# Parts of q and k copied from SBUF to SBUF once a turn instead of through DRAM, with indirect stores, gathers and the ternary layer at other places, in a two-layer transformer kernel

## The chip, the cores and the metric

The kernel runs on one core of a Trainium2 chip. The metric is the device time of one launch in microseconds (us), the median of several runs. The code names the engines so: PE (TensorE, matmuls), DVE (VectorE), ACT (ScalarE), POOL (GpSimd), SP (SyncE, which only issues DMAs here).

## What is computed

Input x is 16 sequences of 512 tokens of 256 numbers. Four residual layers follow each other:

```
x = x + attention0(layernorm(x))   # 16 heads of 16, rotary q and k, window of 128 keys, softmax, output weights
x = x + experts(layernorm(x))      # 8 experts, each token goes to 2 of them: silu(a) * b, gates from a softmax
x = x + attention1(layernorm(x))   # 16 heads of 16, xpos rotary, causal over all 512, biases
x = x + ternary(layernorm(x))      # x @ w.T with w quantised to -1, 0, 1 times a scale
```

The attention scores need nearly float32 accuracy, while the score matmuls take bf16 operands. So q and k are each split into three bf16 parts that add up to the float32 value, and six products of parts are summed by one matmul with a contraction of 6 x 16 = 96 rows.

## The kernel before

The program has three stages. `pipeline` (lines 106 to 1034) runs twice, in the first launch stage as attention0 with the routing of the experts (`routed`, its tiles are a_..., about 0 to 1060 us), and last as attention1 with the sum of the experts' outputs in front and the ternary layer behind (`mixed`, about 2000 to 3335 us). Between them stands `experts`, which the change doesn't touch.

`pipeline` works on one sequence a turn, and several sequences are in the pipeline at once. In turn i the softmax part runs for sequence i (steps "T": the transposed scores k times q plus mask on PE, exp on ACT; steps "PV": probabilities times v on PE), the maxima of the rows for sequence s = i+1 (steps "S": q times k on PE, then the row minimum of the negated scores on DVE, line 839), layer norm, transposition and the projections to q and k for sequence m = i+2, and the output side (o = i-1). The function `turn(i)` (lines 148 to 200) gives each step a position between 0 and 1 in its turn; `merged` sorts them, and every engine runs its own steps in that one order. So a step that waits on an engine holds up all steps behind it there. PE runs the T, PV and S steps, the product to v (`v`), two transpositions of the output (`flip`, line 1017, and `back`, line 1023), the output product (`out`, line 1032), the transposition of the next input (`turn`, line 898), the projections (`project`, line 885) and the transposition of the row maxima (`minus`, line 977).

The parts of q and k of sequence m (a = 0 is q, a = 1 is k) come into the tile `parts` [128, 2, 3, 2, 512] in bf16: 128 partitions are 8 dimensions times 16 heads, 3 parts, 2 halves of the head. The first two parts are casts on ACT (lines 611 and 614), with subtractions on POOL (lines 548 and 552). The S and T matmuls want the 96 rows (which part, which half, which of 8 dimensions) on partitions and the heads along the free axis, in `qst` and `kst` [98, 16, 512], two buffers of each. This change of layout goes through DRAM: the step `store` (lines 461 to 468) writes the parts to `parts_d` in 3 DMAs for q and 6 for k (the order of the parts differs, `STORED`), and the step `stack` (lines 469 to 478) reads them back as 96 partitions, for a group of 4 heads at a time: 8 DMAs of 384 KB a sequence, each of 96 rows of 4 KB. The stacks of groups 0 to 2 stand at 0.70, 0.74 and 0.78 of the turn and that of group 3 at its end; each waits until the T steps of that group of sequence m-2 have left the buffer. The S step of each group waits for its own semaphore `stack_loaded`. The row maxima go into rows 96 and 97 of `qst` the same way, in two DMAs through `nmax_d` (lines 479 to 486).

The S steps of a turn stand evenly between 0.03 and 0.97 (28 of them in attention0, 44 in attention1).

POOL issues the indirect DMAs. In attention0 the 8 `scatter` DMAs of a sequence (line 525) write the normed tokens to the experts' input; they stand at 0.97 of the turn after the sequence's T steps and wait for the row numbers that DVE works out (line 810, position 0.9475). In attention1 the 8 `gather` DMAs (line 532) fetch the experts' outputs in two lots of 4, at 0.35 and 0.81 of a turn, into one tile `yg`; the DVE steps `mix` (line 690) add them to x, lot by lot, and wait for a whole lot of 4 (semaphore `gathered`). The second lot's `mix` stands at 0.94 to 0.985, the statistics of that sequence (line 674) at the start of the next turn.

Of the kernel before, what the change touches and what calls it, by code (L numbers as in the profile page):

```python
# [105 lines left out]
def pipeline(nc, name, x_in, x_out, w_all, w_out, tables, biases, window, scale, consts, routed, mixed, ternary_w):  # L106
# [18 lines left out]
    parts_d = nc.dram_tensor(f"{name}_parts_dram", [2, 2, NR, 2, P, T], BF16, kind="Internal").ap()  # L125
    nmax_d = nc.dram_tensor(f"{name}_nmax_dram", [2, 2, H, T], BF16, kind="Internal").ap()
# [21 lines left out]
    def turn(i):  # L148
# [11 lines left out]
        if 0 <= o < B:  # L160
# [3 lines left out]
            out += [(0.16 + 0.02 * t, ("stats2", o, t)) for t in range(NT)] + [(0.235, ("aggr2", o))]  # L164
            if routed:
                out += [(0.28 + 0.02 * t, ("norm2", o, t)) for t in range(NT)]
                out += [(0.15, ("y", o)), (0.50, ("turn2", o, 0)), (0.52, ("turn2", o, 1)), (0.58, ("score", o)),
                        (0.66, ("exp2", o)), (0.79, ("place", o)), (0.97, ("scatter", o))]
                out += [(0.615 + 0.0175 * k, ("gates", o, k)) for k in range(20)]
            else:  # L170
                out += [(0.27 + 0.015 * t, ("norm2", o, t)) for t in range(NT)]
                out += [(0.345, ("turn2", o, 0)), (0.36, ("turn2", o, 1)), (0.49, ("last", o, 0)), (0.51, ("last", o, 1)),
                        (0.515, ("final", o, 0)), (0.535, ("final", o, 1)), (0.54, ("y", o))]
        if 0 <= s < B:
            lo, hi = 0.03, 0.97
            out += [(lo + (hi - lo) * (k + 0.5) / NS, ("S", s, k // NSG, k % NSG)) for k in range(NS)]
            out += [(0.01, ("v", s)), (0.035, ("vcopy", s, 0)), (0.055, ("vcopy", s, 1)), (0.54, ("minus", s, 0, 0)), (0.68, ("minus", s, 0, 1))]
        for n, at in ((m, -0.5),) * (m == 0) + ((m + 1, 0.55),) * (0 <= m + 1 < B):
            out.append((at, ("load", n)))
            if mixed:  # L180
                out += [(at - 0.2, ("gather", n, 0)), (at + 0.26, ("gather", n, 1))]
                out += [(at + 0.19 + 0.02 * t, ("mix", n, 0, t)) for t in range(NT)]
                out += [(at + 0.39 + 0.015 * t, ("mix", n, 1, t)) for t in range(NT)]
            else:
                out += [(at + 0.25 + 0.02 * t, ("stats", n, t)) for t in range(NT)] + [(at + 0.33, ("aggr", n))]
        if biases and 0 <= m < B:
            out.append((0.50, ("shift", m)))
        if 0 <= m < B:
            if mixed:
                out += [(0.005 + 0.02 * t, ("stats", m, t)) for t in range(NT)] + [(0.075, ("aggr", m))]  # L190
                out += [(0.125 + 0.015 * t, ("norm", m, t)) for t in range(NT)]
            else:
                out += [(0.03 + 0.02 * t, ("norm", m, t)) for t in range(NT)]
            out += [(0.20, ("turn", m, 0)), (0.215, ("turn", m, 1))]
# [8 lines left out]
    for i in range(-2, B + 1):  # L203
# [6 lines left out]
    with ctx:  # L210
# [197 lines left out]
        parts_stored = [sem(f"parts_stored{i}") for i in range(2)]  # L408
        stack_loaded = [[sem(f"stack_loaded{i}{g}") for g in range(NG)] for i in range(2)]
        nmax_stored = sem("nmax_stored")  # L410
# [14 lines left out]
        gathered = sem("gathered")  # L425
# [26 lines left out]
        def _(sp):  # L452
            for st in order:
# [7 lines left out]
                elif st[0] == "store":  # L461
                    m, a = st[1:]
                    sp.wait_ge(part2_done, 2 * m + a + 1)
                    for r, (p0, np_) in enumerate(STORED[a]):
                        src = parts[:, a, p0:p0 + np_]
                        dst = parts_d[m % 2, a, STORED_AT[a][r]:STORED_AT[a][r] + np_]
                        sp.dma_start(dst.rearrange("r b p n -> p (r b) n"), src.rearrange("p r b n -> p (r b) n"))\
# [1033 lines left out]
```

## Time and profile before

| what | us |
|---|---|
| median of 3 runs | 3323.2 |
| lowest and highest run | 3319.46, 3323.53 |
| the profiled execution's own time | 3336.26 |
| span of its trace | 3334.6 |

The profiled execution is 13.1 us longer than the median of the runs, and 1.7 us of its time lie outside the span. In the rows, a timeline row has the start and duration in us, the engine, the line, the operation with its tiles (out<-in) and the number merged into the row; square brackets give the idle time of the engine before it and what ended it. "SPq" is the queue in which SP issues. "PEclk" is the granted clock of PE as a share of 2.4 GHz, and the DMA share is the mean busy share of 16 DMA engines.

### The profile page before, as it was taken

The page shows a single profiled execution, that of the slowest core. Times are in us where ns is not written, and L with a number is a line of the kernel's source. Part 1 is how long each engine was busy: PE and PEld are TensorE (multiplying, and loading weights), DVE is VectorE, ACT ScalarE, POOL GpSimd, SP SyncE. Part 2 cuts the span into 40 slices and gives each one's busy share as a digit, 9 for nine tenths or more (in the row PEclk, how much of TensorE's full clock was granted, in tenths as well). Part 3 has the DMA queues.
Part 4 walks back from the last instruction along what each step waited for, and adds up shares of the span by engine and source line. Part 5 has one row for each costly group of instructions (what it writes and reads, how often), then busy time and mean ns, then how long its engine had stood idle before and what let it go on. Part 6 is the DMA issues. An engine that isn't in the chain of part 4 may idle for free. (4 is left out here: it accounts for less than half of the span.)

```text
span 3334.6 us, 52247 instructions
## 1 busy us (share of the span) xinstructions
PE 2627.1 (79%) x17657; PEld 1777.4 (53%) x17830; DVE 1940.5 (58%) x6550; ACT 1463.5 (44%) x2485; POOL 1140.8 (34%) x919
## 2 busy tenths in 40 slices
PE   2788788888886488888888882588888888887887
PEld 2455555555553377777777771244444444444444
DVE  4667677577673344555554443566666656666661
ACT  1445455454453244344443431145555554455554
POOL 2334434444322233333333323333443333333310
PEclk8899999999997698999999995589998998899998
DMA  4544534435431333333333323533334443333330
GB/s 113 152 123 147 153 110 149 151 110 167 139 97 47 137 133 132 132 123 125 120 130 131 132 82 98 165 96 103 107 108 137 126 126 112 103 103 102 103 90 14
DMA packets 240529, 394.13 MB, mean 118 GB/s; under 512 B 26432, under 2 KB 190272, under 8 KB 235072
## 3 DMA queue, kind: packets, MB, share of 16 engines
q1 hardware_dynamic: 222272, 336.94, 33.3%
q0 software_dynamic: 18048, 54.54, 4.9%
q8 instruction: 115, 1.88, 0.2%
q14 instruction: 94, 0.77, 0.1%
HBM read 230.84 MB, written 160.56 MB: 117 GB/s over the span
## 5 line engine op out<-in xcount | busy, mean ns | idle before, releaser
L839 DVE CUSTOM_DVE_ANT_0 a_junk<-a_bank,a_smask 128x256 bf16<-128x256 f32 (+3 forms) x2048 | 812.6, 435 | 523.9 <-PE a_bank L969 514.6
L636 ACT ACTIVATE a_pr<-a_bank 128x512 f32<-128x512 f32 (+1 forms) x1152 | 635.6, 574 | 690.8 <-PE a_bank L890 507.8
L969 PE MATMUL a_bank<-a_kst,a_qst 96*128 96x256 bf16 (+3 forms) x2048 | 459.5, 299 | 203.8 <-DVE a_nmax L839 147.3
L1255 POOL TENSOR_TENSOR e_wl<-e_w_raw,e_wh 128x2048 fp32r<-128x2048 f32 x80 | 279.0, 3488 | 578.6 <-ACT e_wh L1292 578.6
L991 PE MATMUL a_bank<-a_qst,a_kst 98*128 98x256 bf16 (+3 forms) x2048 | 434.8, 289 | 26.5 <-ACT a_pr L636 23.7
L969 PEld LDWEIGHTS a_bank<-a_kst,a_qst 96*128 96x128 bf16 x2048 | 169.7, 102 | 451.2 <-DVE a_nmax L839 268.1
L1009 PE MATMUL a_bank<-a_pr,a_va 128*32 128x256 f32 (+3 forms) x4096 | 360.1, 429 | 47.3 <-ACT a_pr L636 43.2
L1340 PE MATMUL e_bank<-e_xh,e_wh 128*128 128x512 f32 x640 | 277.9, 434 | 111.5 <-DVE e_gf L1313 103.2
L1313 DVE SCALAR_TENSOR_TENSOR e_gf<-e_bank,e_b,e_sa 128x512 f32<-128x512 f32 x160 | 119.8, 749 | 325.7 <-ACT e_sa L1276 325.1
L890 PE MATMUL a_bank<-a_mask,a_identb 128*128 128x128 bf16 (+2 forms) x979 | 284.8, 291 | 0.0
L1317 DVE TENSOR_TENSOR e_gl<-e_gf,e_gh 128x512 fp32r<-128x512 f32 x160 | 211.0, 1319 | 112.7 <-ACT e_gh L1281 112.7
L1340 PE MATMUL e_bank<-e_xl,e_wh 128*128 128x512 f32 x640 | 271.6, 424 | 0.0
L1340 PE MATMUL e_bank<-e_xh,e_wl 128*128 128x512 f32 x640 | 270.0, 422 | 0.0
L991 PEld LDWEIGHTS a_bank<-a_qst,a_kst 98*128 98x128 bf16 x2048 | 180.6, 100 | 149.2 <-ACT a_pr L636 74.5
L1276 ACT ACTIVATE e_sa<-e_bank,e_b 128x512 f32<-128x512 f32 x160 | 109.6, 685 | 283.4 <-PE e_bank L1340 283.4
L1340 PEld LDWEIGHTS e_bank<-e_xh,e_wh 128*128 128x128 f32 x640 | 131.9, 206 | 154.2 <-DVE e_gf L1313 108.9
L532 POOL DMA_INDIRECT a_yg<-ys,a_yrow x128 | 123.9, 968 | 195.8 <-DVE a_xt L690 136.6
L514 POOL TENSOR_SCALAR a_lean<-a_mv 128x4 f32<-128x4 f32 x32 | 7.7, 240 | 529.2 <-DVE a_mv L702 529.2
L1009 PEld LDWEIGHTS a_bank<-a_pr,a_va 128*32 128x32 f32 x4096 | 84.7, 110 | 181.7 <-issue 89.4
L1354 PE MATMUL e_bank<-e_wh,e_gh 128*128 128x256 f32 x640 | 178.1, 278 | 2.9 <-DVE e_gl L1317 2.9
L1354 PE MATMUL e_bank<-e_wh,e_gl 128*128 128x256 f32 x640 | 177.9, 278 | 0.0
L1354 PE MATMUL e_bank<-e_wl,e_gh 128*128 128x256 f32 x640 | 177.8, 278 | 0.0
(172 smaller groups left out, 5255.0 us busy)
## 6 DMA issues: line engine op xcount, KB each, us to landing
a_parts_dram<-a_parts SPq DMA_DIRECT2D x224, 256.0 KB, 3.9
a_qst<-a_parts_dram SPq DMA_DIRECT2D x128, 384.0 KB, 9.8
a_kst<-a_parts_dram SPq DMA_DIRECT2D x128, 384.0 KB, 10.7
e_w_raw<-in_we SPq DMA_DIRECT2D x40, 1024.0 KB, 6.3
a_parts_dram<-a_parts SPq DMA_DIRECT2D x32, 768.0 KB, 3.8
e_xg<-xs SPq DMA_DIRECT2D x40, 512.0 KB, 3.8
e_w_raw<-in_we SPq DMA_DIRECT2D x40, 512.0 KB, 8.2
ys<-e_yt POOLq DMA_DIRECT2D x40, 512.0 KB, 7.8
```

The costliest lines, as they stand in the source:

```text
L532: pool.indirect_dma_start(yg[:, t, :], None, ys, bass.IndirectOffsetOnAxis(ap=yrow[:, k, m * NT + t:m * NT + t + 1], axis=0))\
L636: nc.scalar.activation(pr[b][:, h:h + per, :], TB_[at % 2][:, 0:per * w].rearrange("p (h w) -> p h w", h=per), ACT.Exp, scale=scale).then_ ...
L839: last = nc.vector.tensor_tensor_reduce(junk[:, at % 2, j * w:(j + 1) * w], SB_[at % 2][:, j * w:(j + 1) * w], smask[:, T - w:T], scale=-1 ...
L890: return nc.tensor.matmul(out, identb[:, :], rhs, start=False, stop=True, skip_group_check=True)
L969: last = nc.tensor.matmul(out[:, j * w:(j + 1) * w], q[0:ROWS, hh, qb * P:(qb + 1) * P], k[0:ROWS, hh, k0:k0 + w], start=True, stop=True)
L991: nc.tensor.matmul(out[:, j * w:(j + 1) * w], k[0:AUG, hh, b * P:(b + 1) * P], q[0:AUG, hh, q0:q0 + w], start=(j == 0), stop=False, skip_g ...
L1009: last = nc.tensor.matmul(PVB[32 * j:32 * (j + 1), q0:q0 + w], va[i % 2][:, b, (g * HG + j) * VW:(g * HG + j) * VW + 32], pr[b][:, j, :], ...
L1255: nc.gpsimd.tensor_tensor(part(wl[m.slot]), part(w_raw[m.slot]), part(wh[m.slot]).bitcast(F32), ALU.subtract).then_inc(wl_done, 1)
L1313: nc.vector.scalar_tensor_tensor(gf[f % 2][:, :], BB[f % 2][:, :], b1[s.slot][:, FC + f:FC + f + 1], sa[f % 2][:, :], ALU.add, ALU.mult).t ...
L1317: nc.vector.tensor_tensor(gl[s.slot][:, f, :], gf[f % 2][:, :], gh[s.slot][:, f, :].bitcast(F32), ALU.subtract).then_inc(gl_done, 1)
L1340: last = nc.tensor.matmul(out[:, :], first(w[s.slot])[:, kc, col:col + P], x[s.slot][:, kc, :], start=(p == 0), stop=(p == 3 * KC - 1))
L1354: last = nc.tensor.matmul(YB[n][:, (t % 2) * D:(t % 2 + 1) * D], x[s.slot][:, f, t * P:(t + 1) * P], second(w[s.slot])[:, f, :], start=(p ...
```

## The change

The parts go from `parts` straight to `qst` and `kst`. One DMA copies one part and half, 128 partitions of 1 KB, to 8 partitions with 16 heads of 1 KB each: 12 DMAs for q and 12 for k a sequence, 24 of 128 KB. They all stand at the end of the turn, wait until all T steps of sequence m-2 are done, and raise one semaphore; the first S step of the sequence waits for all 24. The S steps stand between 0.20 and 0.98. The row maxima take one DMA instead of two. `parts_d` and `nmax_d` go. The scatters, which stood at 0.97 of a turn, stand one by one at 0.115 to 0.213 of the next. In attention1 the load of x moves from 0.55 to 0.435, the gathers stand one by one at 0.27 to 0.345 and 0.57 to 0.645, each of the 4 rows of `yg` with a semaphore of its own, the second lot of `mix` at 0.72 to 0.78, the statistics at 0.80 to 0.86 of the same turn, and the ternary layer goes forward (`last` from 0.49 to 0.37, `y` from 0.54 to 0.42).

```diff
             if routed:
                 out += [(0.28 + 0.02 * t, ("norm2", o, t)) for t in range(NT)]
-                        (0.66, ("exp2", o)), (0.79, ("place", o)), (0.97, ("scatter", o))]
+                        (0.66, ("exp2", o)), (0.79, ("place", o))]
...
-                out += [(0.27 + 0.015 * t, ("norm2", o, t)) for t in range(NT)]
-                out += [(0.345, ("turn2", o, 0)), (0.36, ("turn2", o, 1)), (0.49, ("last", o, 0)), (0.51, ("last", o, 1)),
-                        (0.515, ("final", o, 0)), (0.535, ("final", o, 1)), (0.54, ("y", o))]
+                out += [(0.235 + 0.015 * t, ("norm2", o, t)) for t in range(NT)]
+                out += [(0.31, ("turn2", o, 0)), (0.325, ("turn2", o, 1)), (0.37, ("last", o, 0)), (0.385, ("last", o, 1)),
+                        (0.40, ("final", o, 0)), (0.415, ("final", o, 1)), (0.42, ("y", o))]
+        if routed and 0 <= i - 2 < B:
+            out += [(0.115 + 0.014 * k, ("scatter", i - 2, k)) for k in range(2 * NT)]
         if 0 <= s < B:
-            lo, hi = 0.03, 0.97
+            lo, hi = 0.20, 0.98
...
-            out += [(0.01, ("v", s)), (0.035, ("vcopy", s, 0)), (0.055, ("vcopy", s, 1)), (0.54, ("minus", s, 0, 0)), (0.68, ("minus", s, 0, 1))]
+            out += [(0.01, ("v", s)), (0.035, ("vcopy", s, 0)), (0.055, ("vcopy", s, 1)), (0.63, ("minus", s, 0, 0)), (0.75, ("minus", s, 0, 1))]
-        for n, at in ((m, -0.5),) * (m == 0) + ((m + 1, 0.55),) * (0 <= m + 1 < B):
+        for n, at in ((m, -0.5),) * (m == 0) + ((m + 1, 0.55 if routed else 0.435),) * (0 <= m + 1 < B):
             out.append((at, ("load", n)))
             if mixed:
-                out += [(at - 0.2, ("gather", n, 0)), (at + 0.26, ("gather", n, 1))]
-                out += [(at + 0.19 + 0.02 * t, ("mix", n, 0, t)) for t in range(NT)]
-                out += [(at + 0.39 + 0.015 * t, ("mix", n, 1, t)) for t in range(NT)]
+                for t in range(NT):
+                    out += [(at - 0.165 + 0.025 * t, ("gather", n, 0, t)), (at + 0.125 + 0.02 * t, ("mix", n, 0, t)),
+                            (at + 0.135 + 0.025 * t, ("gather", n, 1, t)), (at + 0.285 + 0.02 * t, ("mix", n, 1, t)),
+                            (at + 0.365 + 0.02 * t, ("stats", n, t))]
+                out.append((at + 0.465, ("aggr", n)))
...
             for a in range(2):
-                p = 0.27 + 0.13 * a
+                p = 0.24 + 0.19 * a if mixed else 0.27 + 0.13 * a
-                        (p + 0.15, ("part", m, a, 0)), (p + 0.21, ("part", m, a, 1)), (p + 0.27, ("store", m, a))]
-            out += [(0.70 + 0.04 * g, ("stack", m, g)) for g in range(NG - 1)] + [(1.0, ("stack", m, NG - 1))]
+                        (p + 0.15, ("part", m, a, 0)), (p + 0.21, ("part", m, a, 1)), (0.995 + 0.001 * a, ("stack", m, a))]
...
                 elif st[0] == "stack":
                     m, a = st[1:]
                     sp.wait_ge(part2_done, 2 * m + a + 1)
+                    sp.wait_ge(t_done, max(0, (m - 1) * NS))
+                    dst = (qst, kst)[a][m % 2]
                     for r, (p0, np_) in enumerate(STORED[a]):
+                        for p in range(np_):
+                            for b in range(2):
+                                at = ((STORED_AT[a][r] + p) * 2 + b) * (DH // 2)
+                                sp.dma_start(dst[at:at + DH // 2, :, :], parts[:, a, p0 + p, b, :])\
+                                    .then_inc(stack_loaded[m % 2], 16)
                 elif st[0] == "minus" and st[3] == 1:
...
+                    sp.dma_start(qst[s % 2][ROWS:AUG, half * H // 2:(half + 1) * H // 2, :], nmt[half][:, :])\
                         .then_inc(nmax_loaded[s % 2][half], 16)
...
                 elif st[0] == "scatter":
-                    r = st[1]
+                    r, k, t = st[1], st[2] // NT, st[2] % NT
                     pool.wait_ge(rows_done, r + 1)
...
-                    pool.wait_ge(mixed_in, NT * (2 * m + k))
+                    pool.wait_ge(mixed_in, max(0, NT * (2 * m + k - 1) + t + 1))
...
-                        act.wait_ge(parts_stored[a], 16 * len(STORED[a]) * m)
+                        if m:
+                            act.wait_ge(stack_loaded[(m - 1) % 2], 16 * 4 * NR * ((m - 1) // 2 + 1))
                         nc.scalar.copy(parts[:, a, 0], qk[:, a]).then_inc(part0_done, 1)
...
-                        dve.wait_ge(gathered, 16 * NT * (2 * m + k + 1))
+                    dve.wait_ge(gathered[t], 16 * (2 * m + k + 1))
...
-                    if n == 0:
-                        pe.wait_ge(stack_loaded[s % 2][g], 32 * (s // 2 + 1))
+                    if (g, n) == (0, 0):
+                        pe.wait_ge(stack_loaded[s % 2], 16 * 4 * NR * (s // 2 + 1))
```

## Rows read from the trace of the kernel before

**Rows 1.** The page: busy time of each engine, share of the span, instructions.

```profile
PE 2627.1 (79%) x17657; PEld 1777.4 (53%) x17830; DVE 1940.5 (58%) x6550; ACT 1463.5 (44%) x2485; POOL 1140.8 (34%) x919
```

**Rows 2.** Windows: one turn of attention0 in two stretches, one of attention1.

```profile
core 0: us, PE busy (x) PEld busy (x) DVE busy (x) ACT busy (x) POOL busy (x), PEclk, DMA share, GB/s
582.90:606.90 24.00, 17.89 (x128) 13.18 (x131) 9.54 (x50) 9.50 (x19) 9.12 (x11) 0.86 0.62 194
606.90:644.30 37.40, 33.66 (x293) 20.58 (x297) 33.22 (x150) 21.22 (x38) 15.73 (x14) 1.00 0.33 104
...
2520.40:2544.50 24.10, 18.48 (x123) 11.50 (x123) 12.05 (x49) 10.63 (x21) 1.71 (x4) 0.86 0.37 91
2544.50:2594.80 50.30, 43.44 (x303) 23.73 (x305) 36.76 (x130) 27.44 (x50) 25.20 (x21) 0.93 0.39 119
```

**Rows 3.** Timeline of PE, attention0: the drain of one turn.

```profile
568.11 0.38 PE L969 MATMUL a_bank<-a_kst,a_qst 96*128 96x256 bf16 x2
568.32 0.38 PE L991 MATMUL a_bank<-a_qst,a_kst 98*128 98x256 bf16 x2
...
582.49 0.38 PE L890 MATMUL a_bank<-a_mask,a_identb 128*128 128x512 bf16 x1
...
595.77 1.12 PE L1023 MATMUL a_bank<-a_ident,a_on 128*128 128x128 f32 x4 [5.47 <-issue]
...
597.65 3.71 PE L1032 MATMUL a_bank<-a_wo,a_ot 128*128 128x256 f32 x8 [0.34 <-ACT a_ot L652]
...
601.86 1.89 PE L1032 MATMUL a_bank<-a_wo,a_ot 128*128 128x256 f32 x8
...
606.55 0.39 PE L977 MATMUL a_bank<-a_identb,a_nparts 128*16 128x128 bf16 x4
```

**Rows 4.** Timeline of POOL, attention0: the first and the last of 8 scatters.

```profile
585.05 1.09 POOL L525 DMA_INDIRECT xs<-a_rn,a_row  x1 [0.67 <-DVE a_row L810]
...
594.03 0.96 POOL L525 DMA_INDIRECT xs<-a_rn,a_row  x1 [0.30 <-issue]
```

**Rows 5.** Timeline of DVE, attention1: the wait for the second lot of gathers.

```profile
2527.75 0.88 DVE L690 SCALAR_TENSOR_TENSOR a_xt<-a_yg,a_gate,a_xt 128x256 f32<-128x256 f32 x2 [6.64 <-issue]
```

**Rows 6.** Groups of DVE, attention1, ten turns (2312.6 to 3060.1 us).

```profile
L690 DVE SCALAR_TENSOR_TENSOR a_xt<-a_yg,a_gate,a_xt 128x256 f32<-128x256 f32 x80 | 36.8, 481 | 62.8 <-issue 62.8
...
L674 DVE BATCH_NORM_STATS2 a_stats<-a_xt 128x6 f32<-128x256 f32 x40 | 15.9, 418 | 0.0
```

**Rows 7.** Windows of rows 2, line 839 alone: DVE busy, PEclk, DMA.

```profile
582.90:606.90 24.00, 5.68 (x34) 0.86 0.62 194
...
2520.40:2544.50 24.10, 6.43 (x29) 0.86 0.37 91
```

**Rows 8.** Windows (columns of rows 2): DMA at the parts' store, then the maxima's load and store.

```profile
574.00:578.00 4.00, 3.67 (x47) 2.06 (x48) 3.90 (x26) 1.76 (x4) 0.00 (x0) 1.00 1.08 381
...
548.70:549.05 0.35, 0.35 (x4) 0.26 (x3) 0.35 (x3) 0.00 (x0) 0.26 (x2) 1.00 0.11 47
547.15:547.40 0.25, 0.25 (x4) 0.10 (x1) 0.25 (x3) 0.00 (x0) 0.00 (x0) 1.00 0.27 66
```

**Rows 9.** Timeline of SP's queue: 16 loads of 16 KB in a row.

```profile
3.91 7.38 SPq L333 DMA_DIRECT2D a_wo<-in_wo  x16
```

**Rows 10.** Line 482, the store of the row maxima, 16 KB.

```profile
DMA to landing us min/median/max: 1.4/2.0/4.4
```

**Rows 11.** Timeline: the last part and the first S, attention0, then attention1.

```profile
53.94 2.12 POOL L552 TENSOR_TENSOR a_parts<-a_qk,a_parts 128x1024 bf16<-128x1024 f32 x1 [1.16 <-ACT a_parts L614]
69.78 1.04 PE L969 MATMUL a_bank<-a_kst,a_qst 96*128 96x128 bf16 x6 [20.85 <-DMA a_kst<-a_parts_dram]
...
2083.63 2.12 POOL L552 TENSOR_TENSOR a_parts<-a_qk,a_parts 128x1024 bf16<-128x1024 f32 x1 [1.16 <-ACT a_parts L614]
2099.49 1.03 PE L969 MATMUL a_bank<-a_kst,a_qst 96*128 96x128 bf16 x6 [26.90 <-DMA a_kst<-a_parts_dram]
```

More of the change, by code:

```diff
@@ L163, in turn @@
                     (0.145, ("add", o, 1))]
-            out += [(0.16 + 0.02 * t, ("stats2", o, t)) for t in range(NT)] + [(0.235, ("aggr2", o))]
+            if routed:
+                out += [(0.16 + 0.02 * t, ("stats2", o, t)) for t in range(NT)] + [(0.235, ("aggr2", o))]
+            else:
+                out += [(0.155 + 0.015 * t, ("stats2", o, t)) for t in range(NT)] + [(0.21, ("aggr2", o))]
             if routed:
@@ L188, in turn @@
         if 0 <= m < B:
[L189 to L194, printed above, removed]
+            out += [(0.03 + 0.02 * t, ("norm", m, t)) for t in range(NT)]
+            out += [(0.18 if mixed else 0.20, ("turn", m, 0)), (0.195 if mixed else 0.215, ("turn", m, 1))]
             for a in range(2):
-                p = 0.27 + 0.13 * a
+                p = 0.24 + 0.19 * a if mixed else 0.27 + 0.13 * a
                 out += [(p, ("project", m, a)), (p + 0.04, ("rope", m, a, 0)), (p + 0.065, ("rope", m, a, 1)),
-                        (p + 0.15, ("part", m, a, 0)), (p + 0.21, ("part", m, a, 1)), (p + 0.27, ("store", m, a))]
-            out += [(0.70 + 0.04 * g, ("stack", m, g)) for g in range(NG - 1)] + [(1.0, ("stack", m, NG - 1))]
+                        (p + 0.15, ("part", m, a, 0)), (p + 0.21, ("part", m, a, 1)), (0.995 + 0.001 * a, ("stack", m, a))]
         return out
     order = []
-    for i in range(-2, B + 1):
+    for i in range(-2, B + 2):
         order += merged([turn(i)])
@@ L407, in pipeline @@
         x_loaded = [sem(f"x_loaded{i}") for i in range(RING)]
-        parts_stored = [sem(f"parts_stored{i}") for i in range(2)]
-        stack_loaded = [[sem(f"stack_loaded{i}{g}") for g in range(NG)] for i in range(2)]
-        nmax_stored = sem("nmax_stored")
+        stack_loaded = [sem(f"stack_loaded{i}") for i in range(2)]
         nmax_loaded = [[sem(f"nmax_loaded{i}{half}") for half in range(2)] for i in range(2)]
@@ L424, in pipeline @@
         scattered = [sem(f"scattered{i}") for i in range(2)]
-        gathered = sem("gathered")
+        gathered = [sem(f"gathered{t}") for t in range(NT)]
         mixed_in = sem("mixed_in")
@@ L460, in _ @@
                         .then_inc(x_loaded[m % RING], 16)
[L461 removed]
+                elif st[0] == "stack":
                     m, a = st[1:]
                     sp.wait_ge(part2_done, 2 * m + a + 1)
+                    sp.wait_ge(t_done, max(0, (m - 1) * NS))
+                    dst = (qst, kst)[a][m % 2]
                     for r, (p0, np_) in enumerate(STORED[a]):
[L465 to L478 removed]
+                        for p in range(np_):
[3 more added lines that the diff above has]
+                                    .then_inc(stack_loaded[m % 2], 16)
                 elif st[0] == "minus" and st[3] == 1:
```

39 lines of the change are left out of this document (10 added, 29 removed).

## The prediction

> **What bounds the kernel now.** The page first: PE is busy for 79% of the span, DVE for 58%, and no engine is full [rows 1]. So a share is no answer, and I cut a turn at the point the change touches: the end of the last T step of a sequence, since from there the copies may start. The first stretch runs from there to the transposition of the maxima at position 0.205; I call it the drain, and it is where the change takes the S steps out. The rest of the turn is the main stretch. In attention0 they take 24.0 and 37.4 us (61.4 a turn), in attention1 24.1 and 50.3 (74.4) [rows 2]. In the main stretch of attention0 DVE is busy 33.2 of 37.4 us and PE 33.7: both are nearly full, and the stretch can't shrink much. In the drain PE is busy 17.9 of 24.0 us at a mean granted clock of 0.86, in attention1 18.5 of 24.1 at 0.86, and DVE about half or less. Here the time lies open.
>
> Why: in attention0 PE stands idle for 5.47 us before line 1023, put down to nothing in the trace, and afterwards works at 1.2 GHz: the same eight records of line 1032 take 3.71 us and, a little later, 1.89 [rows 3]. The gap lies inside the 8 scatters on POOL, from 585.05 to 595.0 us [rows 4], which meet the last stack loads. In attention1 DVE waits 6.64 us for the second lot of gathers [rows 5], 62.8 us in ten turns [rows 6], with S steps queued behind, and PE runs dry. The loads themselves end no wait but the first one of each layer [rows 11].
>
> **What the change removes.** Six S steps leave the drain of attention0 and nine that of attention1. On PE one takes 0.21 us (568.11 to 568.32 [rows 3]), so 1.3 and 1.9 us. On DVE line 839 takes 5.68 and 6.43 us there [rows 7]. PE's necessary drain is its busy time, less what the low clock cost (0.14 of 24 us: 3.4), less these: 17.9 - 3.4 - 1.3 = 13.2 and 18.5 - 3.4 - 1.9 = 13.2 us. With about 1 us of short waits between ACT and PE I take 14 for both. That needs the two waits above gone. The gathers of attention1 leave the turn's end (to 0.65 at the latest, their `mix` 0.075 of a turn, 5 us, later), so the 6.64 us go. In attention0 the scatters don't in fact move: POOL has nothing between its last norm step at 0.88 and them, and their only wait, for the row numbers, ends at 0.95 in either kernel. What changes is what they meet: copies that stay inside SBUF instead of loads. I take the idle time as gone, and keep the other case as a rival.
>
> **What it adds: the copies.** The first S waits for all 24, PE is in order, and so T and PV steps queue behind it. Three prices, after the last T:
> - Issue. 16 small loads in a row took 7.38 us of SP, 0.46 each [rows 9]; 24 take 11.1 us. Nothing that is due is behind them on SP: the maxima's second half is issued at 0.205 and needed at 0.5.
> - Data. A busy DMA engine moved 381 / (16 x 1.08) = 22.0 GB/s in pieces of 1 KB [rows 8]. How many engines share a copy into 8 partitions no row shows, but the load into 2 partitions kept 0.11 x 16 = 1.8 engines busy [rows 8], so I take one for each partition: 8 engines. 3.146 MB / (8 x 22.0) = 17.9 us. With 16 engines it is 8.9, less than the issue.
> - Fixed. The shortest store of 16 KB took 1.4 us to land [rows 10].
>
> So the copies take 17.9 + 1.4 = 19.3 us; below, 11.1 + 1.4 = 12.5 (16 engines), above, see the third rival. I take 19.3, since the row with 2 partitions is nearest. It is more than PE's 14: the drain becomes 19.3 us, set by the copies.
>
> **The main stretch.** It gets the S steps and, in attention1, four `mix` at 0.481 and four statistics at 0.418 us [rows 6]. DVE there: 33.2 + 5.0 = 38.2 us, and 36.8 + 5.7 + 3.6 = 46.1 (one S of about 0.7 us stays in the drain). At the fullness of attention0's stretch, 33.2 / 37.4 = 0.89, that is 43 and 52; full, 38.2 and 46.1. I take 41 and 50: near the upper ends, the second helped by the 3.5 us that the clock of 0.93 cost it [rows 2].
>
> **The small edits at nothing.** The maxima lose a store and a wait, hidden by half a turn of T steps. The parts' store to DRAM goes; POOL and ACT wait for the copies of the turn before, over by 0.39. The ternary steps and `y` come earlier; what waits for `y` is only the load, needed a quarter of a turn on. If those covers went, PE would see some 2 us of landing.
>
> **The start of each layer.** From the last part to the first S now 69.78 - 56.06 = 13.7 us, and 99.49 - 85.75 = 13.7 [rows 11]; the part ends 2.12 after its start. With the copies 19.3: +5.6 twice.
>
> **Sum.** Attention0: 19.3 + 41 = 60.3 against 61.4, -1.1. Attention1: 69.3 against 74.4, -5.1. Fifteen full turns of each have copies, S and T: 15 x -6.2 = -93, plus 11 is -82 us. On the profiled execution's 3336.3 that gives 3254, and as the median of the runs is 13.1 lower, 3241.
>
> **Rivals.** Each by the same sum.
> - *All 16 engines share a copy.* Then it takes 12.5 us and PE's 14 set the drain: 55 and 64, -16.8 a pair, -252 and 2 less at the starts: 3069. For: with issue spread over 11 us the placing of S at 0.20 would just fit. Against: the two-partition row. Chance 0.17.
> - *The scatter gap stays.* Drain of attention0 24.0 - 1.3 = 22.7, a turn 63.7 (+2.3); attention1 as before: -42 + 11 = -31: 3292. Chance 0.10.
> - *Neighbouring partitions get in each other's way (slower).* All 8 target partitions of a copy are neighbours. The maxima's store reads 16 neighbouring partitions, and there an engine moved 66 / (16 x 0.27) = 15.3 GB/s instead of 22.0 [rows 8]. At that pace: 3.146 MB / (8 x 15.3) = 25.7, plus 1.4 is 27.1. Turns 68.1 and 77.1: +6.7 + 2.7, x 15 = 141, and 27 at the starts: 3491. The sign turns where the copies take 21.9 us. Against: the pair of engines that wrote to 2 neighbours moved 47 / 1.76 = 26.7 GB/s each. Chance 0.22.
> - *They block each other wholly.* If four neighbours share the pace of one engine at its best, a copy runs at 2 x 26.7 GB/s: 58.9 + 1.4 = 60.3 us, turns 101 and 110, +1137 and 93: 4553. For it speaks only the 16-partition row, and weakly; engines that fall out of step would reach other partitions. Chance 0.08. The Trainium skill states this as a rule (SBUF — State Buffer, "Door 1: The DMA port swizzle"): four neighbouring partitions hang on one port of 27.2 GB/s, so 8 give 54 GB/s. By it the copies take 58 + 1.4 us and this case is the forecast. The trace's pair of writers went past it over 16 KB, which is too short to settle a stream.
> - *DVE bounds the main stretch.* S squeezed into 0.78 of the turn makes it 45.1 and 55: +3.0 and -0.1: +43 + 11: 3377. Chance 0.08.
> - That the change does nothing measurable, cases in between: 0.05.
>
> **How the numbers follow.** The forecast has 0.30, with a range of its own of 3190 to 3290. Faster (beyond 0.2%, 7 us, about what a measurement of this kernel can tell): 0.30 + 0.10 + 0.17, less 0.01 of edges. Slower: 0.22 + 0.08 + 0.08, less 0.01. The range reaches from the first rival to the third with some margin, 3060 to 3510; outside lie the blocked copies and the tails of both.
>
> **What would show it.** Right: from the first copy's issue to the first S some 20 us; DMA share near 0.5 in that time; PE idle before line 969 by 4 to 6 us a turn, ended by a copy of `qst` or `kst`; no wait of line 690 above 1 us; turns of 60 and 69 us. DMA share 1 and no PE wait: first rival. Share 0.5 for 27 us or more: the third or fourth. A gap inside the scatters beyond the copies' end: the second. A main stretch over 44 us in attention0 with DVE above 0.93: the last. Wrong as a whole would be a gain that comes from the main stretch.

## The result, and the profile after

| kernel | median, us | lowest to highest | span of the profiled execution | granted clock |
|---|---|---|---|---|
| before | 3323.36 | 3319.46 to 3325.27 (4 runs) | 3334.6 | 0.893 |
| after | 4331.88 | 4319.11 to 4341.16 (4 runs) | 4317.4 | 0.805 |

The ratio is 1.3025, with an interval of 1.2996 to 1.3055: 1008 us slower, far outside the range. The changed kernel has other line numbers: the S matmuls are line 956 (969 before), their row minimum 826 (839), `back` 1010 (1023), `out` 1019 (1032), the copies 468.

The page's engines after, against [rows 1]. PE is busy 114 us longer for the same matmuls (173 of their records are missing before), which goes with the lower clock, and has 63% of a longer span.

```profile
PE 2741.4 (63%) x17830; PEld 1790.8 (41%) x17830; DVE 1914.6 (44%) x6550; ACT 1471.8 (34%) x2485; POOL 1143.5 (26%) x919
```

The waits of PE and of DVE (engine line waited for: us in total, times, longest). One wait stands out, and it comes once a sequence and layer, 32 times:

```profile
PE a_bank L956 <- DMA a_kst<-a_parts: 868.8, 32, 40.3
...
DVE a_junk L826 <- PE a_bank L956: 1172.5, 281, 39.6
```

One turn of attention0, PE's timeline. The gap inside the scatters is still there (4.48 us, against 5.47 in [rows 3]), the eight records after it still take 3.75 us, and then PE waits 28.84 us more for the last copy.

```profile
680.69 1.12 PE L1010 MATMUL a_bank<-a_ident,a_on 128*128 128x128 f32 x4 [4.48 <-issue]
...
682.57 3.75 PE L1019 MATMUL a_bank<-a_wo,a_ot 128*128 128x256 f32 x8 [0.77 <-ACT a_ot L639]
...
720.20 0.61 PE L956 MATMUL a_bank<-a_kst,a_qst 96*128 96x128 bf16 x4 [28.84 <-DMA a_kst<-a_parts]
```

SP's queue in that turn. The issue of the copies takes 34 us, not 11, and the store of x and a copy of maxima stand behind it. The issue goes by the pace of the pieces: the same 24 issues take 16.5 us in the spread kernel below, and the 24 loads of the kernel through DRAM, with 8 pieces each instead of 128, take 8 to 9. That a full queue holds SP up would fit this; no run shows the queue itself.

```profile
667.34 13.43 SPq L468 DMA_DIRECT2D a_qst<-a_parts  x12
680.87 20.70 SPq L468 DMA_DIRECT2D a_kst<-a_parts  x12
701.67 2.97 SPq L479 DMA_DIRECT2D x<-a_xt  x1
704.69 2.78 SPq L473 DMA_DIRECT2D a_qst<-a_nmt  x1
```

Windows (columns of [rows 2]): a turn of attention0, cut at the first S, one of attention1 cut likewise, and then two stretches with copies alone.

```profile
667.30:720.20 52.90, 17.02 (x117) 11.96 (x116) 6.00 (x23) 10.16 (x19) 8.15 (x10) 0.65 0.60 89
720.20:764.80 44.60, 39.50 (x311) 23.20 (x311) 34.82 (x176) 21.35 (x37) 16.61 (x15) 0.88 0.05 14
3060.10:3107.20 47.10, 16.80 (x120) 10.68 (x120) 5.82 (x16) 11.54 (x23) 0.00 (x0) 0.70 0.53 68
3107.20:3165.30 58.10, 49.50 (x310) 25.04 (x310) 43.45 (x163) 26.43 (x48) 27.24 (x25) 0.86 0.12 37
...
708.00:716.00 8.00, 0.00 (x0) 0.00 (x0) 0.00 (x0) 0.00 (x0) 0.00 (x0) 0.50 0.58 63
...
3070.00:3100.00 30.00, 9.78 (x59) 5.50 (x57) 3.99 (x8) 5.05 (x10) 0.00 (x0) 0.67 0.57 71
```

From the first copy to the first S pass 52.9 and 47.1 us. The DMA share is near 0.57, about 9 of 16 engines, as the forecast had it; but they move 63 to 71 GB/s. A busy engine moves 63 / (16 x 0.58) = 6.8 and 71 / (16 x 0.57) = 7.8 GB/s, where the forecast had 22.0. In the trace's records of single pieces, one of 1 KB takes 147 ns on average from 684 to 700 us and 131 from 3070 to 3100, in the parts' store before the change 46.

The first S of each layer, against the two S rows of [rows 11]: it comes 32.7 us later at the start of attention0.

```profile
102.50 0.61 PE L956 MATMUL a_bank<-a_kst,a_qst 96*128 96x128 bf16 x4 [40.26 <-DMA a_kst<-a_parts]
...
2584.10 1.04 PE L956 MATMUL a_bank<-a_kst,a_qst 96*128 96x128 bf16 x6 [14.31 <-DMA a_kst<-a_parts]
```

Cut at the first and last S of each layer, the two spans differ so: start of attention0 +32.7 us, its S steps from first to last +438.3 (933.9 to 1372.2), from there to the first S of attention1, with the experts between, +13.6, its S steps +501.2 (1153.9 to 1655.1), the rest -2.9; together +982.8, the difference of the spans. Steady turns have 89.7 and 109.5 us, 61.6 and 74.8 before (means of 9 to 11).

### The profile page after: what moved, and what is told of

It is laid out like the page before. It is cut to its first block and busy times, and to the rows that moved or that the text cites. A ratio compares the mean times of both kernels' runs of the same rounds, so it can differ in the third digit from the quotient of the medians.

```text
span 4317.4 us, 52556 instructions
## 1 busy us (share of the span) xinstructions
PE 2741.4 (63%) x17830; PEld 1790.8 (41%) x17830; DVE 1914.6 (44%) x6550; ACT 1471.8 (34%) x2485; POOL 1143.5 (26%) x919
## 5 line engine op out<-in xcount | busy, mean ns | idle before, releaser
L956 PE MATMUL a_bank<-a_kst,a_qst 96*128 96x256 bf16 (+3 forms) x2048 | 485.5, 314 | 1052.3 <-DMA a_kst<-a_parts 868.8
L978 PE MATMUL a_bank<-a_qst,a_kst 98*128 98x256 bf16 (+3 forms) x2048 | 455.6, 300 | 33.9 <-ACT a_pr L623 33.2
L996 PE MATMUL a_bank<-a_pr,a_va 128*32 128x256 f32 (+3 forms) x4096 | 388.8, 457 | 29.7 <-issue 18.2
L877 PE MATMUL a_bank<-a_mask,a_identb 128*128 128x512 bf16 (+2 forms) x1152 | 367.1, 319 | 0.0
L978 PEld LDWEIGHTS a_bank<-a_qst,a_kst 98*128 98x128 bf16 x2048 | 192.1, 106 | 151.7 <-ACT a_pr L623 81.7
L860 DVE TENSOR_TENSOR a_xt<-a_bank,a_xt 128x512 f32<-128x512 f32 x64 | 44.3, 692 | 368.2 <-PE a_bank L1019 363.6
L526 POOL TENSOR_TENSOR a_qk<-a_rt 128x512 f32<-128x512 f32 x64 | 81.5, 1273 | 426.1 <-DVE a_rt L815 240.7
```

The lines of the kernel that those rows point to most:

```text
L877: return nc.tensor.matmul(out, identb[:, :], rhs, start=False, stop=True, skip_group_check=True)
L956: last = nc.tensor.matmul(out[:, j * w:(j + 1) * w], q[0:ROWS, hh, qb * P:(qb + 1) * P], k[0:ROWS, hh, k0:k0 + w], start=True, stop=True)
L978: nc.tensor.matmul(out[:, j * w:(j + 1) * w], k[0:AUG, hh, b * P:(b + 1) * P], q[0:AUG, hh, q0:q0 + w], start=(j == 0), stop=False, skip_g ...
L996: last = nc.tensor.matmul(PVB[32 * j:32 * (j + 1), q0:q0 + w], va[i % 2][:, b, (g * HG + j) * VW:(g * HG + j) * VW + 32], pr[b][:, j, :], ...
```

## The experiments

**Chips.** The runs were made on several chips, and the kernel before takes 3316 to 3341 us on some and 3245 to 3263 on others. Each ratio below is against the kernel before on the same chip, and the theories in the expectations are: A, neighbours share a way into SBUF; B, the reads from `parts` collide; C, a copy inside SBUF is slow in itself.

### Which side of the copies is slow

Spread kernel, an edit in the step `stack`:

```diff
-                                at = ((STORED_AT[a][r] + p) * 2 + b) * (DH // 2)
-                                sp.dma_start(dst[at:at + DH // 2, :, :], parts[:, a, p0 + p, b, :])\
+                                at = (STORED_AT[a][r] + p) * 2 + b
+                                sp.dma_start(dst[at:ROWS:2 * NR, :, :], parts[:, a, p0 + p, b, :])\
```

> The changed kernel, with one edit: the 8 rows that a copy writes lie 12 partitions apart instead of side by side (row n + 12 d instead of 8 n + d, in both stacks, so the products are the same). Bytes, pieces of 1 KB, issue and order stay. Theory A (the neighbours share a way into SBUF, four to one): the pieces, 146 ns each in the changed kernel, fall to about 47 ns, the copies of a sequence take some 20 us from the first issue to the first S instead of 44 and 51, and the time lies between 3241 (the forecast's sum) and 3520 (4332 less 15 turns of 24 + 30 us). Theory B (the reads from the parts' tile collide) and theory C (a copy inside SBUF is slow in itself): nothing changes, 4330 and 146 ns.

Two apart:

```diff
+                                n = (STORED_AT[a][r] + p) * 2 + b
+                                at = n // 2 * DH + n % 2
+                                sp.dma_start(dst[at:at + DH:2, :, :], parts[:, a, p0 + p, b, :])\
```

> As the spread kernel, but the 8 rows of a copy lie 2 apart (16 (n // 2) + n % 2 + 2 d), so that a group of four neighbouring partitions gets two of them instead of four. Theory A: a piece takes about half of 146 ns, 73, the copies 3.146 MB at 8/73 ns per KB = 112 GB/s, 28 us, plus 1.4; the time lies in the middle between the changed and the spread kernel, nearer to the spread one. Theories B and C: 4330 and 146 ns.

Through DRAM, read back into 8 neighbours a time:

```diff
+                    rows = parts_d[m % 2, a].rearrange("r b p n -> (r b p) n").rearrange("(d h) n -> d h n", h=H)
+                    for n in range(2 * NR):
+                        at = n * (DH // 2)
+                        sp.dma_start(dst[at:at + DH // 2, :, :], rows[at:at + DH // 2, :, :])\
+                            .then_inc(stack_loaded[m % 2], 16)
```

> The changed kernel, but the parts are stored to DRAM as before (0.27 of a turn after the projection) and read back at the end of the turn in 24 loads of 128 KB, each into 8 neighbouring partitions like the copies. Theory A (the writing side): the loads keep the pace of the copies, some 44 and 51 us from the first issue to the first S, and the time is within 3% of 4332. Theories B and C (the reading side, or SBUF to SBUF in itself): the loads run at 8 engines' full pace or better, 20 us or less, and the time is 3520 or less.

| kernel | us | to the kernel before on that chip | first copy (or load) to first S, attention0 / 1 |
|---|---|---|---|
| after, first chip | 4331.88 | 1.3025 | 46.3 / 51.7 |
| DRAM, 8 neighbours | 4178.19 (1 run) | 4178.19 / 3252.27 = 1.285 | 41.7 / 45.7 |
| two apart | 3752.08 (1 run) | 3752.08 / 3252.27 = 1.154 | 29.5 / 32.6 |
| spread, 12 apart | 3466.18 | 1.0669 (1.0625 to 1.0714) | 26.7 / 20.9 |

Windows inside a burst of attention1: the spread kernel, then two apart, then through DRAM.

```profile
3176.00:3192.00 16.00, 13.10 (x76) 8.80 (x71) 1.79 (x7) 7.53 (x15) 0.00 (x0) 0.79 0.51 168
```

```profile
3160.00:3180.00 20.00, 13.74 (x73) 7.95 (x70) 4.96 (x12) 9.93 (x20) 0.00 (x0) 0.83 0.56 109
```

```profile
3815.00:3850.00 35.00, 11.84 (x68) 6.86 (x68) 4.07 (x9) 9.24 (x19) 0.00 (x0) 0.70 0.51 74
```

The DMA share is the same in all, 0.51 to 0.58; what moves is 168, 109, and 71 to 74 GB/s. A busy engine moves 168 / (16 x 0.51) = 20.6 GB/s when the rows are 12 apart, which is the 22.0 of the forecast. Reading from `parts` is the same in the spread kernel and in the slow one, so B falls; it is also a copy inside SBUF, so C falls; and loads from DRAM into 8 neighbours crawl like the copies. That run was 3.4% under the 4327 that the changed kernel takes elsewhere, a little past the 3% of the expectation. A stands in this: the limit is on the writing side, and goes by how many neighbouring rows are written at one time. That the neighbours share in groups of four is not shown by these three: groups of eight with twice the pace would give the same, since 8 rows side by side lie in one such group, rows 2 apart in two, rows 12 apart in eight. Only 1, 2 and 12 apart were tried.

The Trainium skill (SBUF — State Buffer, "Door 1: The DMA port swizzle") has groups of four as a rule: four neighbouring partitions share a port of 27.2 GB/s. By it two ports give 54 GB/s (2 x 27.2, an estimate) and four give 109. The trace agrees for the rows two apart (109), and for neighbours shows more than the 54, namely 63 to 80. That one copy overlaps the next, which writes to other rows, would explain this; it was not tried by itself.

### Scatters and copies on the same engines

Both kernels hold a scatter back until PE is at its place in the turn:

```diff
-            out += [(0.115 + 0.014 * k, ("scatter", i - 2, k)) for k in range(2 * NT)]
+            out += [(0.30 + 0.08 * k, ("scatter", i - 2, k)) for k in range(2 * NT)]
...
                     pool.wait_ge(rows_done, r + 1)
+                    pool.wait_ge(t_done, min(B * NS, (r + 2) * NS + int(NS * (0.28 + 0.08 * st[2]))))
```

> The changed kernel, unchanged, beside the kernel before on the chip of these runs. If the excess is the copies' alone, it is as large here as on the first chip, some 1000 us: 4230 to 4330.

> The kernel with copies to rows 12 apart (3466 us), with the scatters of attention0 taken out of the copies' way: one by one at 0.30 to 0.86 of the turn. If the 25 to 27 us from the first copy to the first S in attention0, where attention1 has 21.6, come from the scatters on the same DMA engines, they become 20 to 22 and the time is 45 to 90 us less. If not (PE's own drain or the issue sets them), the time stays, or is up to 20 us more, as with the paced scatters alone.

> The changed kernel with the same paced scatters. In its trace the pieces of the copies take 146 ns, but 55 to 61 while scatters run. If the scatters help by bringing the DMA engines out of step, so that they write to other groups of neighbours at one time, then without them each burst in attention0 takes the 50 to 54 us of attention1 instead of 36 to 54, and the time is some 50 to 150 us more. If the scatters only compete with the copies, it is 50 us less or more.

The changed kernel took 4327.36 on the second kind of chip, 1.3271 (1.3241 to 1.3301): the same time as on the first, though the kernel before is 2% faster there. The paced spread kernel took 3401.78, 1.0446 (1.0430 to 1.0462), 64 us less than the spread one (73 by the ratios, since the two ran on different chips), and its burst in attention0 fell from 26.7 to 21.1 us, as in attention1. Pacing the changed kernel did the opposite, 4406.79 (one run), with 51.3 us a burst instead of 47.2. The waits of PE for the copies, changed kernel then paced:

```profile
PE a_bank L956 <- DMA a_kst<-a_parts: 962.4, 32, 39.8
```

```profile
PE a_bank L957 <- DMA a_kst<-a_parts: 1010.3, 32, 40.3
```

Bursts of one run vary from 35 to 54 us, so the 4 us are a difference of means of 14; the 79 us of the whole agree with them, when some 20 are taken off for what pacing costs elsewhere (see the kernel before with paced scatters below). So with the rows spread the scatters compete with the copies, and with neighbouring rows they help. That they do it by bringing the engines out of step fits pieces of 58 ns on average while the last of them run (679 to 683 us), but was not tried by itself.

### What the new order is worth without slow copies

The changed order with two fast loads of 96 rows, all else of the change alone, and the place of the S steps alone:

```diff
+                    sp.dma_start(dst[0:ROWS, :, :], rows).then_inc(stack_loaded[m % 2], 16)
```

> The changed kernel's order, with its parts through DRAM and back in 2 loads of 96 partitions at the end of the turn (1.57 MB each, all 16 engines). It tells what the place of the S steps and of the other moved steps is worth without slow copies. At the 381 GB/s of the parts' store 3.146 MB take 8.3 us; with 2 us of landing the first S comes some 10 to 12 us after the issue, PE's own drain of 14 us then sets it, and the turns are 55 and 64 us by the forecast's sum, 3070 in all; if the order itself costs something (DVE full with the S steps in 0.78 of a turn, or the scatters' gap that stays), it is 3290 to 3380. Theory A, B and C agree here.

> The kernel before, unchanged, for its trace on the chip of the runs beside it: its time equals that of the kernel before there, and the turns are 61 and 74 us within the ratio of the two chips.

> The kernel before with all of the change but the copies and the place of the S steps: parts and maxima through DRAM, S from 0.03 to 0.97, and the new places of the scatters, gathers, mix, statistics and of the ternary layer. If the wait of 6.6 us for the second lot of gathers was on the path, attention1 has turns of 70 us instead of 74.4 and the time is 40 to 65 us less than before. If another wait takes its place (PE is short of granted clock there), it is within 15 us of before. Attention0 is as before, since POOL issues the scatters at the same moment in both.

```diff
-            lo, hi = 0.03, 0.97
+            lo, hi = 0.20, 0.98
...
-(0.54, ("minus", s, 0, 0)), (0.68, ("minus", s, 0, 1))]
+(0.63, ("minus", s, 0, 0)), (0.75, ("minus", s, 0, 1))]
```

> The kernel before with one part of the change: the S steps from 0.20 to 0.98 of a turn (and the maxima's transpositions at 0.63 and 0.75), all else as before. On this chip the changed order with fast loads was 74 us slower than before, and the other moved steps alone 14 us faster. If the place of the S steps is what costs, this kernel is 70 to 90 us slower. If the loads at the turn's end cost it, this one is within 20 us of before. By the forecast (main stretch 41 and 50 us, drain 14 where nothing else is late) it would be over 100 us faster.

The last two add one edit, to the kernel with S late and to the rest-only kernel:

```diff
-                    sp.dma_start(nmax_d[s % 2, half], nmt[half][:, :]).then_inc(nmax_stored, 16)
...
+                    sp.dma_start(qst[s % 2][ROWS:AUG, half * H // 2:(half + 1) * H // 2, :], nmt[half][:, :])\
```

> The kernel with the S steps from 0.20 to 0.98 alone (110 us slower than before), and with the row maxima copied straight into their stack instead of through DRAM. If the S steps' own place costs some 88 us (74 us slower for the whole changed order with fast loads, 14 us faster for the other moved steps), the wait for the maxima (91 us) was in its shadow and this kernel is 70 to 100 us slower than before. If the whole excess was that wait, it is within 20 us of before. By the forecast's sum it would be over 100 us faster.

> The kernel with all of the change but the copies and the place of the S steps (14 us faster than before), and with the row maxima copied straight into their stack. The maxima have half a turn there, so no wait goes: 10 to 18 us faster than before, as without it. If the store and load through DRAM cost more than their own wait (they share queues with the parts), it is 20 us or more.

| kernel | us | ratio (interval) |
|---|---|---|
| before again | 3256.32 (1 run) | 1.001 |
| changed order, fast loads | 3326.65 | 1.0225 (1.0200 to 1.0250) |
| rest only | 3239.79 | 0.9955 (0.9943 to 0.9968) |
| rest only, maxima direct | 3242.68 | 0.9966 (0.9952 to 0.9979) |
| S late only | 3365.64 | 1.0344 (1.0319 to 1.0369) |
| S late, maxima direct | 3337.61 | 1.0262 (1.0242 to 1.0283) |

Moving the S steps costs 84 us by itself. With the loads at the turn's end it is 88, worked out from two runs: 74 slower for the whole order, 14 faster for the rest. The windows of the kernel before on that kind of chip (drain and main stretch of attention0, then of attention1), below them those with S late and the maxima direct, and then those of the changed order with fast loads:

```profile
604.90:622.30 17.40, 15.17 (x124) 11.44 (x127) 9.04 (x48) 8.82 (x18) 9.04 (x10) 1.00 0.82 256
622.30:660.20 37.90, 33.98 (x297) 20.80 (x301) 33.72 (x152) 21.72 (x40) 15.85 (x14) 1.00 0.36 114
2515.10:2539.70 24.60, 18.63 (x124) 11.46 (x125) 11.44 (x47) 10.15 (x20) 1.71 (x4) 0.86 0.39 99
2539.70:2590.30 50.60, 43.49 (x306) 23.84 (x313) 37.38 (x132) 27.96 (x52) 25.20 (x21) 0.93 0.42 125
```

```profile
657.70:676.10 18.40, 16.03 (x115) 11.39 (x115) 5.41 (x23) 8.77 (x17) 8.25 (x10) 0.91 0.65 183
676.10:719.20 43.10, 37.83 (x314) 22.34 (x313) 35.05 (x177) 22.42 (x39) 16.42 (x15) 0.92 0.42 130
2521.60:2545.10 23.50, 17.92 (x112) 12.36 (x112) 7.93 (x25) 10.09 (x20) 1.71 (x4) 0.85 0.42 99
2545.10:2596.10 51.00, 43.09 (x319) 23.34 (x318) 38.69 (x153) 27.79 (x51) 25.21 (x21) 1.00 0.39 116
```

```profile
721.20:739.40 18.20, 15.71 (x111) 11.32 (x112) 5.30 (x22) 8.70 (x17) 8.14 (x10) 0.91 0.88 242
739.40:782.60 43.20, 37.48 (x310) 22.39 (x315) 35.15 (x177) 22.48 (x39) 16.50 (x15) 0.92 0.29 95
2520.60:2540.60 20.00, 16.74 (x116) 10.69 (x116) 4.04 (x13) 10.29 (x21) 0.00 (x0) 0.91 0.68 159
2540.60:2596.80 56.20, 47.67 (x311) 24.19 (x314) 45.10 (x167) 27.50 (x50) 27.24 (x25) 0.88 0.30 95
```

These are single turns, and turns differ by a microsecond or two; what follows are means of ten. In attention0 the drain gets no shorter without its six S steps, 18.7 us against 18.6. PE is idle there for 2.4 us in both. The 1.3 us of the S steps went, and the granted clock fell from 0.965 to 0.909, which is an estimated 0.056 x 18.7 = 1.0 us. The main stretch grows from 37.3 to 42.6 us. PE is busy 3.7 us more in it: 1.3 for the six S steps, and most of the rest the clock, which falls from 1.00 to 0.93; its waits for DVE's row minimum grow from 2.0 to 3.8 us a turn. DVE is busy for 35.0 of the 42.6 us, so it isn't full.

In attention1 the drain loses 1.2 us (25.0 to 23.8) and the main stretch gains as much (49.9 to 51.0), so the turn stays at 74.9 and 74.7. From the first S of a layer to its last, attention0 takes 81 us longer and attention1 6 us less: the whole cost stands in attention0. The changed order with fast loads has 18.7 and 42.7 us there too, and in attention1 20.5 and 54.5. Why the clock falls was not tried.

The kernel with S late and the maxima through DRAM was 26 to 28 us worse. Its PE waits 90.8 us for the maxima in all, of which the direct copy leaves 50.2.

The rest-only kernel lost most of the wait of [rows 5] (line 690 waits 26.4 us in all, against 152.2 in the kernel before on that kind of chip) and gained only 14 us. Its turns of attention1 are no shorter, 74.7 us against 74.9: the drain falls from 25.0 to 21.2, and the main stretch grows from 49.9 to 53.5. Two views of it, DVE and then POOL, at the same moment of a turn of attention1:

```profile
2563.03 0.47 DVE L690 SCALAR_TENSOR_TENSOR a_xt<-a_yg,a_gate,a_xt 128x256 f32<-128x256 f32 x1
...
2564.52 2.66 DVE L690 SCALAR_TENSOR_TENSOR a_xt<-a_yg,a_gate,a_xt 128x256 f32<-128x256 f32 x1
```

```profile
2564.76 2.13 POOL L548 TENSOR_TENSOR a_qk<-a_qk,a_parts 128x1024 f32<-128x1024 f32 x1
```

One `mix` a turn takes 2.66 us instead of 0.48 and lies over a subtraction on POOL; before the change no `mix` met one. The Trainium skill (SBUF — State Buffer, "Who interferes with whom") says that a VectorE instruction with two SBUF inputs and a GpSimd one that reads SBUF lock each other out; the trace agrees in that the mix ends only 0.29 us after the subtraction. The mix had begun 0.24 us before it, and the subtraction keeps its 2.13 us, so the one that begins later need not be the one that waits.

### Moving the mixes

Both are the rest-only kernel with one number changed, 0.50 and 0.47:

```diff
-        for n, at in ((m, -0.5),) * (m == 0) + ((m + 1, 0.55 if routed else 0.435),) * (0 <= m + 1 < B):
+        for n, at in ((m, -0.5),) * (m == 0) + ((m + 1, 0.55 if routed else 0.50),) * (0 <= m + 1 < B):
```

> The rest-only kernel (14 us faster than before), with the load of x, the gathers, mixes and statistics of attention1 0.065 of a turn later, so that the first lot of mixes comes when POOL has begun its last tensor_tensor or is through. If the 2.66 us mix was what gave the gain back, all mixes take 0.48, the turn of attention1 is 2.2 us shorter (72.9), and the time 30 us less than that of the rest-only kernel. If DVE has slack there, it is within 8 us of it. If the later gathers come late again, it is slower.

> The same with half the shift (0.035 of a turn later than in the rest-only kernel). It is a second place between the two: if the mixes that lie over POOL's tensor_tensors are what counts, its time goes with their number and length in its own trace; if not, it is within 8 us of the rest-only kernel.

> The mix-clear kernel once more (49 us faster than before on a chip where the kernel before takes 3329 and has the gap during the scatters in both). Its gain stands in attention1, so on a chip without the gap the ratio is the same within half a per cent, 0.985, and the time 3205; if the gain hangs on the gap, it is above 0.99.

At 0.50: 3280.06, 0.9859 (0.9834 to 0.9883), and again 3277.14, 0.9833 (0.9807 to 0.9860). At 0.47: 3289.54, 0.9882 (0.9860 to 0.9905). Both chips were of the kind where the kernel before takes 3320 to 3335, so whether the ratio holds on the other kind stays open. The gain stands in attention1, though: from its first S to its last it takes 1107 and 1123 us, the rest-only kernel 1151, and the kernel before 1154 and 1155 on the two kinds of chip. Turns of attention1 have 71.8 and 72.7 us (means of ten), in the rest-only kernel 74.7. But the lock is not what went: at 0.50 the long `mix` still takes some 1.8 us, and at 0.47 it takes some 2.9, more than before the shift, while the turn is 2.0 us shorter all the same. PE's granted clock over a turn goes the same way, 0.95 at 0.50, 0.93 at 0.47 and 0.91 in the rest-only kernel; but the kernel with S late and the maxima direct has 0.96 with turns of 74.7, so the clock alone doesn't set the turn. The mix is held up beside POOL, the price of that is unsettled, and what of the new place helps was not found.

### The gap inside the scatters

The kernel before, with its scatters paced by the edit shown above, then the same with the rest of the change:

> The kernel before, with its 8 scatters of a turn no longer in a row at the turn's end but one by one at 0.30 to 0.86 of the next, each held back until PE has done the T steps of that place. If PE's idle time before the back transposition (5.47 us) and the low clock after it come from the scatters in a row, both go, the turn of attention0 is 5.5 to 9 us shorter, and the time 80 to 135 us less than before. If each scatter holds PE up wherever it stands, eight pieces of 0.7 us take the gap's place and the time stays within 15 us. If the gap comes from the stack loads at the turn's end, it stays where it is.

> Both of the last two together: the sum of their gains, 120 to 200 us less than before, if each stands in its own layer; the parts go through DRAM as before.

These ran on a chip where the kernel before takes 3254, and were slower: 3276.66, 1.0062 (1.0048 to 1.0076), and 3269.10, 1.0043 (1.0029 to 1.0056). The trace of the kernel before there says why: there is no gap to take away, and the main stretch of attention0 grows by 1.5 us a turn with the scatters in it (37.3 to 38.8). Its two rows that answer to [rows 3]:

```profile
613.68 0.65 PE L1023 MATMUL a_bank<-a_ident,a_on 128*128 128x128 f32 x4 [1.54 <-ACT a_ot L652]
615.10 1.97 PE L1032 MATMUL a_bank<-a_wo,a_ot 128*128 128x256 f32 x8 [0.55 <-ACT a_ot L652]
```

The mix-clear kernel and the same one paced ran on a chip with the gap:

> The mix-clear kernel with the paced scatters. On a chip with the gap: if the scatters in a row make it, drains of attention0 fall from 22.5 to 17 us and the time is 60 to 85 us less than that of the mix-clear kernel. If each scatter makes PE wait wherever it stands, there is no gain. On a chip without the gap: 15 to 25 us more than the mix-clear kernel, as the paced scatters alone.

Unpaced, then paced (`back` and `out` of one turn):

```profile
720.58 1.11 PE L1023 MATMUL a_bank<-a_ident,a_on 128*128 128x128 f32 x4 [5.49 <-issue]
...
722.46 3.72 PE L1032 MATMUL a_bank<-a_wo,a_ot 128*128 128x256 f32 x8 [0.34 <-ACT a_ot L652]
```

```profile
636.57 0.66 PE L1024 MATMUL a_bank<-a_ident,a_on 128*128 128x128 f32 x4 [1.54 <-ACT a_ot L653]
638.00 1.97 PE L1033 MATMUL a_bank<-a_wo,a_ot 128*128 128x256 f32 x8 [0.55 <-ACT a_ot L653]
```

The gap and the low clock behind it are gone, the drain of attention0 falls from 24.1 to 18.9 us (means of ten turns, cut at the end of the last T step and of the maxima's transposition), its main stretch grows from 37.3 to 39.7, and the kernel takes **3233.04 us, 0.9701 (0.9674 to 0.9727)**: the fastest, 44 us under the unpaced one; the expectation had 60 to 85, since it left out what pacing costs the main stretch. So the scatters in a row at the turn's end make the gap, on the chips that have it. The stack loads from DRAM that they meet there aren't needed for it: the changed kernel has none and keeps a gap of 4.48 us. The edit spaces the scatters and moves them at once, and which of the two counts was not tried. Why some chips have no gap stays open.

## Why the prediction was wrong

- **Bytes per engine: the step that failed.** "3.146 MB / (8 x 22.0) = 17.9 us": the number of engines was right (share 0.57, and 20.6 GB/s an engine with the rows spread), but 22.0 GB/s came from a store to DRAM, whose pieces come from 128 partitions. Into 8 neighbours the engines moved 6.8 to 7.8 GB/s each, and the copies took 46.3 and 51.7 us instead of 19.3.
- **The rival had it, at 0.08.** "They block each other wholly", with turns of 101 and 110 and 4553 us, was the mechanism; measured were 89.7 and 109.5, and 4332. The term mis-sized in it is the 60.3 us of a burst, which measured 46.3 and 51.7; that copies overlap at their seams and the scatters help in attention0 would explain it. What spoke for the low chance was the writer pair at 26.7 GB/s each over two neighbours [rows 8]: two engines on one group of four would have been 53 GB/s, but that row covers 16 KB in 0.35 us. Why it went so fast stays open; a row so short was weak ground for the pace of a stream of 3 MB.
- **"PE's necessary drain is 14."** With the S steps gone it is 18.7 us in attention0 and 20.5 to 23.8 in attention1. In attention0 the busy time at full clock came out near the 13.2 of the sum (16.3 less an estimated 0.09 x 18.7 = 1.7 for the clock, 14.6); what the sum lacked are 2.4 us of idle time, where it had 1, and those 1.7 us, where it had none. This would have made the forecast wrong by itself: with fast loads the order is 74 us slower, not 82 faster. That run was on the kind of chip without the gap, where the kernel before has less to lose.
- **The main stretch of 41 and 50** came to 42.7 and 54.5 us in the changed order with fast loads, and to 42.6 and 51.0 with S late alone. "At the fullness of attention0's stretch" had given 43 and 52, but that it fits attention0 is luck: DVE's share there is 0.82, not the 0.89 of the estimate, and what grew is PE's busy time, by a lower clock above all, and PE's waits for the row minimum.
- **"I take the idle time as gone."** On the first chip the gap stayed, 4.48 us, inside the copies' wait, so it cost nothing there: on the other kind of chip the changed kernel takes the same time.
- **"The 6.64 us go."** They went, and a main stretch as much longer took their place; at 0.435 the rest of the change brought 14 us, at 0.50 some 50 on the other kind of chip. In the changed kernel itself three `mix` a turn take 1.2 to 1.9 us instead of 0.48.
- **Issue at 11.1 us** was 34, as it goes by the pace of the pieces. It ended nothing, since the copies were the bound.
- **The starts, +5.6 each**, were +32.8 and +21.7, from the end of the last part to the first S (35.4 us in attention1, from 2548.66), by the same pace.

## What to carry to other kernels

Before a layout change is moved from DRAM to SBUF, count how many neighbouring partitions the bytes in flight are written to at one time, and spread the rows of one DMA if the consumer allows it: the same bytes took 21 us instead of 52 in attention1. When work is moved out of a stretch, its busy time is not what the stretch gets shorter by: here six S steps left, and a lower granted clock took back what they had cost, so the clock and the idle time of the stretch that is left need a price of their own. Cut both layers at the same two events and take means of many turns, for single turns differ by more than the effect. Indirect DMAs issued in a row can go with a gap on PE on one chip and not on another, so a gain from pacing them must be measured on both.

## What the runs showed of the hardware that was not expected

- Pieces of 1 KB written by 8 engines to 8 neighbouring partitions took 131 to 147 ns each on average, two apart 76 to 83, 12 apart 50; from DRAM, 16 KB pieces into neighbours took 1.78 us.
- The kernel before is 2% faster on some chips than on others. Of the 80 us, 74 are in attention0, 61.6 against 55.8 us a turn, where PE stands 5.5 us before `back` in a row of 8 scatters on the slower kind and 1.5 on the other. With the scatters held apart it is 1.5 on the slower kind too.
- More traffic made a burst shorter: with 8 scatters in its middle the copies took 47.2 us on average, without them 51.3 (one run).
- Taking 1.3 us of matmuls out of a stretch of 18.6 us left it as long, with PE's granted clock at 0.91 instead of 0.97.
- A VectorE instruction of 0.48 us took 2.66, and at another place 2.87, beside a GpSimd `tensor_tensor` of 2.13.
